# A routed mixture-of-experts kernel: row lists in five groups (1, 1, 2, 4 and 8 experts) instead of three, a third scatter buffer, one gather moved behind later scatters

## The chip, the cores and the metric

The kernel runs on one core of one Trainium2 chip. The metric is the device time of one execution in microseconds (us), lower is better.

## The reference

Input x is 2 x 1024 tokens of 128 channels in f32. A first sublayer (two wavelet levels and linear attention) gives x1; after a layer norm the tokens h go through a routed feed-forward layer, in which each of 16 experts picks its own 256 tokens:

```python
    x = x + _L0_attn_ref(_layernorm(x, axis=-1), ...)
    x = x + _L0_ffn_ref(_layernorm(x, axis=-1), ...)

        scores = jax.nn.sigmoid(h @ gate_w.T)
        cap = math.ceil(T / E * TOP_K)                        # 2048 / 16 * 2 = 256
        topk_score, topk_ids = jax.lax.top_k(scores.T, cap)   # per expert
        xin = h[topk_ids]
        up = jnp.einsum('ecd,efd->ecf', xin, up_w) + up_b[:, None, :]
        g = jnp.einsum('ecd,efd->ecf', xin, gw) + gb[:, None, :]
        eo = jax.nn.silu(g) * up
        eo = jnp.einsum('ecf,edf->ecd', eo, down_w) + down_b[:, None, :]
        flat = (eo * topk_score[..., None]).reshape(-1, Dm)
        out = jnp.zeros_like(h).at[topk_ids.reshape(-1)].add(flat)
        shared = silu(x @ sh_gate_w.T) * (x @ sh_up_w.T)
        return out + shared @ sh_down_w.T
```

The inner width is 512 (four tiles of 128), that of the shared expert 256 (two tiles).

## The kernel before, in words

Each engine (PE, the matmul engine; DVE; ACT; POOL; SP) has its own program, written out by hand, and they meet at semaphores. Nothing is scheduled by a tool: an engine runs its list in order, and a wait holds up all that stands behind it.

**Up to the routing.** The first 82 us make x1, the normalized rows with their scores (stored to DRAM as `h_rows`), and a bitwise search for each expert's 256th highest score. Meanwhile the shared expert runs for the first three quarters of the tokens.

**Row lists.** For every token and expert the rank matmuls leave a slot number, 0 to 255, in PSUM (two copies; ACT copies one to `slot_a`, DVE takes the larger of the two). To turn slots into lists of row numbers, a group of n experts goes through these steps: DVE cuts each slot into a low and a high digit of base 16 and makes one-hot rows of them (`hot_lo`, `hot_hi`), with the token's number multiplied into the low ones (`times_token`); PE multiplies high by low over 16 blocks of tokens into a table of 16n x 16n (`table`, 16 matmuls); DVE keeps the blocks that belong to one expert, sums them and spreads them (`lay_table`, three dependent instructions); PE brings them into slot order (`spread`, one matmul); DVE converts them to integers in `rows` (`slot_rows`). Only then can POOL gather rows for the experts of the group. The groups are of 4, 4 and 8 experts. The steps of group 0 and 1 come before the expert loop, those of group 2 are put between the steps of its first 17 tiles. In the same stretch the shared expert's last quarter is finished (`shared_up`, the product `sh_hid`, `shared_down`, `add_shared`), after which SP stores the last quarter of out.

**Expert loop.** An expert e has four inner tiles j; q = 4e + j counts them. For each q PE does the up and the gate product (L1434, L1435), ACT the silu (L734), DVE the gated product (L1086), and PE two tiles later the down product (L1415). In tile j = 2 PE turns the next expert's gathered rows (`turn_x`, L1402) and DVE copies them (`keep_x`, L1064). When an expert's four down products are done, DVE adds the bias into a buffer `eo` (`add_bias`, L1074), ACT weighs it by the scores (`weigh`, L563, two halves), and POOL scatters it, adding into out (L542, two halves). For the last expert, `add_bias(14)`, `turn_x(15)` and `keep_x(15)` come directly before its tile 60 (`FINAL`).

**POOL's list** sets the order of all gathers and scatters. A gather fetches 128 rows, so there are two per expert and 32 in all, into seven buffers. First come 12 (experts 0 to 5), then per expert its two scatters and `BETWEEN[e]` more gathers:

```python
            def scatter(e):
                if e == 0:
                    pool.wait_ge(s_store, 16 * (NT // 4))
                else:
                    pool.wait_ge(s_scat, 16 * CH * e)
            ...
            for e in range(E):
                scatter(e)
                for _ in range(BETWEEN[e]):
                    gather(*divmod(chunk, CH))
                    chunk += 1
```

So a scatter waits until all scatters before it have landed (they add into the same rows). There are two `eo` buffers: `add_bias(e)` waits until scatter e - 2 has landed.

## Time and profile before

| | |
|---|---|
| median of 3 timed runs | 206.1 us (206.09 to 206.11) |
| profiled execution, first to last instruction | 204.6 us |
| left between the two, around the span | 1.5 us |
| PE busy | 181.2 us (89%), 1196 records |
| DVE busy | 125.5 us (61%) |
| ACT busy | 90.3 us (44%) |
| POOL busy | 127.5 us (62%) |
| mean granted TensorE clock | 0.966 |

The profiled execution has no time of its own besides its span; the 1.5 us by which the timed runs are longer lie outside the first and last instruction. A row of a timeline gives start, duration, engine, line and operation, destination<-source, shape and count, and in brackets the idle time before it with what ended that. PEclk is the granted share of TensorE's full clock (1.00 is 2.4 GHz, 0.50 is 1.2 GHz). Line numbers are those of the kernel before.

### The profile page before, as it was taken

To read this page: it belongs to the slowest core of one execution; us is meant where nothing else is said; L and a number is where in the kernel's file an instruction comes from. 1 tells how busy PE (TensorE), PEld (TensorE's weight loads), DVE (VectorE), ACT (ScalarE), POOL (GpSimd) and SP (SyncE) were. 2 spreads that over 40 slices of the span, in tenths; PEclk is the share of its full clock that TensorE was granted. 3 is DMA by queue.
4 is the path that set the end of the run, shared out by engine and by line. 5 is a ranking of instruction groups with operands and counts; after the bars stand their busy time and mean duration, and the time that the engine had idled before them with its cause. 6 is when DMAs were issued, how large, how long until landed. Compare 5 with 4: busy or idle time off the path is not lost.

```text
span 204.6 us, 3620 instructions
## 1 busy us (share of the span) xinstructions
PE 181.2 (89%) x1196; PEld 156.4 (76%) x1196; DVE 125.5 (61%) x430; ACT 90.3 (44%) x239; POOL 127.5 (62%) x195
## 2 busy tenths in 40 slices
PE   6979898999979999998999999999999999957800
PEld 6947688999936677857899999999999889945700
DVE  4888999999878787785667644454445344422300
ACT  0687512448697768110344344444444345422210
POOL 7494005556117475927777888878878777866660
PEclk9999999999999999999999999999999999995875
DMA  5599999800030271104313323333233333332221
GB/s 149 182 411 419 420 419 419 363 12 3 0 117 0 99 225 51 49 23 138 91 44 42 43 42 45 54 40 42 43 47 53 40 40 29 40 40 21 20 24 13
DMA packets 11649, 22.26 MB, mean 109 GB/s; under 512 B 1504, under 2 KB 8800, under 8 KB 11504
## 3 DMA queue, kind: packets, MB, share of 16 engines
q1 hardware_dynamic: 5968, 17.52, 22.7%
q0 software_dynamic: 5664, 4.53, 16.1%
q8 instruction: 9, 0.15, 0.3%
q14 instruction: 8, 0.07, 0.1%
HBM read 17.72 MB, written 4.33 MB: 108 GB/s over the span
## 4 chain that ended last, share of the span: by engine, by line
PE 41%; DMA 15%; POOL 14%; issue 11%; DVE 10%; ACT 4%; POOLq 1%; SPq 1%; DVEq 0%; ACTq 0%
DMA out_dram<-area,rows 13%; POOL out_dram L542 9%; PE bank L1155 7%; PE bank L1434 4%; PE bank L1110 4%; PE bank L1435 4%; POOL hT L531 4%; PE bank L1296 4%; PE bank L1415 3%; PE bank L1308 3%; DMA x_tok<-in_x_dram 2%; PE bank L1258 2%; DVE junk L950 1%; DVE area L807 1%; DVE hT L817 1%
## 5 line engine op out<-in xcount | busy, mean ns | idle before, releaser
L542 POOL DMA_INDIRECT out_dram<-area,rows x32 | 50.7, 1584 | 16.8 <-DMA out_dram<-area,rows 8.7
L1086 DVE SCALAR_TENSOR_TENSOR area<-bank,consts,sgate 128x256 f32<-128x256 f32 x64 | 30.9, 483 | 42.4 <-ACT sgate L734 42.1
L734 ACT ACTIVATE sgate<-bank,consts 128x256 f32<-128x256 f32 x64 | 30.3, 473 | 53.3 <-PE bank L1435 53.1
L1434 PE MATMUL bank<-area,wT 128*128 128x256 f32 x128 | 40.3, 397 | 4.8 <-issue 4.1
L1415 PEld LDWEIGHTS bank<-wT,area 128*128 128x128 f32 x256 | 38.1, 191 | 4.1 <-DVE area L1086 1.0
L531 POOL DMA_INDIRECT hT<-h_rows,rows x32 | 31.9, 995 | 12.7 <-issue 9.1
L1435 PE MATMUL bank<-area,wT 128*128 128x256 f32 x128 | 39.3, 390 | 0.0
L1415 PE MATMUL bank<-wT,area 128*128 128x128 f32 x256 | 38.6, 275 | 0.6 <-DVE area L1086 0.6
L1435 PEld LDWEIGHTS bank<-area,wT 128*128 128x128 f32 x128 | 25.2, 197 | 3.7
L1434 PEld LDWEIGHTS bank<-area,wT 128*128 128x128 f32 x128 | 20.5, 198 | 6.2 <-issue 5.7
L518 POOL TENSOR_TENSOR sh_hid<-sh_up,sgate 128x64 f32<-128x64 f32 x48 | 13.7, 322 | 14.6 <-ACT sh_up L686 12.1
L1110 PE MATMUL bank<-ident 128*128 128x128 f32 x132 | 19.2, 304 | 1.6 <-POOL ident L411 1.6
L1110 PEld LDWEIGHTS bank<-ident 128*128 128x128 f32 x132 | 17.8, 215 | 2.1 <-POOL ident L411 1.6
L1155 PE MATMUL bank<-sh_hid,area 128*128 128x128 f32 x160 | 18.6, 276 | 0.0
L1155 PEld LDWEIGHTS bank<-sh_hid,area 128*128 128x128 f32 x160 | 18.2, 192 | 0.3 <-ACT area L609 0.3
L1296 PE MATMUL bank<-hT,sh_wT 128*128 128x512 f32 x32 | 17.3, 629 | 0.6 <-ACT hT L650 0.6
L563 ACT ACTIVATE area<-area,hT 128x128 f32<-128x128 f32 x32 | 11.0, 392 | 10.3 <-DVE area L1074 10.3
L950 DVE TENSOR_SCALAR_CACHE_REDUCE junk<-area,search 128x256 bf16<-128x256 f32 (+1 forms) x30 | 13.2, 477 | 1.3 <-ACT area L664 0.8
L491 POOL TENSOR_TENSOR x_tok<-x_tok,consts 128x128 f32<-128x128 f32 x4 | 3.2, 816 | 15.1 <-DVE area L873 15.1
L1074 DVE TENSOR_TENSOR area<-bank,x_tok 128x256 f32<-128x256 f32 x16 | 6.7, 419 | 9.0 <-DMA out_dram<-area,rows 8.2
L1308 PEld LDWEIGHTS bank<-sh_wT,sh_hid 128*128 128x128 f32 x64 | 8.4, 191 | 4.4 <-issue 3.3
L446 POOL TENSOR_TENSOR rstd<-var_eps,half_pow 128x4 f32<-128x4 f32 (+1 forms) x6 | 7.4, 1232 | 6.6 <-DVE var_eps L762 6.6
(195 smaller groups left out, 259.1 us busy)
## 6 DMA issues: line engine op xcount, KB each, us to landing
wT<-in_weights_dram SPq DMA_DIRECT2D x16, 768.0 KB, 16.2
h_rows<-hrow SPq DMA_DIRECT2D x2, 576.0 KB, 3.7
x_tok<-in_x_dram SPq DMA_DIRECT2D x4, 256.0 KB, 3.9
x_tok<-in_down_b_dram SPq DMA_DIRECT2D x1, 1024.0 KB, 6.2
out_dram<-x SPq DMA_DIRECT2D x4, 256.0 KB, 2.1
hT<-h_rows,rows POOLq DMA_INDIRECT x32, 2.6
out_dram<-area,rows POOLq DMA_INDIRECT x32
sh_wT<-in_shared_dram SPq DMA_DIRECT2D x1, 384.0 KB, 2.9
```

The costliest lines, as they stand in the source:

```text
L531: pool.indirect_dma_start(out=gath[:, e % GBUF, c, :], out_offset=None, in_=h_rows[:, :], in_offset=bass.IndirectOffsetOnAxis(ap=rows[:, c ...
L542: pool.indirect_dma_start(out=out_rows, in_=eo[:, e % 2, c, :], in_offset=None, out_offset=bass.IndirectOffsetOnAxis(ap=rows[:, c, e:e + 1 ...
L734: act.activation(sgate_e[:, q % SGB, :], up_bank(q)[:, CAP:2 * CAP], ACT.Silu, bias=biasT[:, 1, j, e:e + 1]).then_inc(s_sil, 1)
L950: last = dve.tensor_scalar(junk[:, k, :], keys, cand[:, k:k + 1], 0.0, ALU.is_ge, ALU.add, accum_out=cnt[:, k:k + 1])
L1086: dve.scalar_tensor_tensor(hidden[:, e % 2, j, :], up_bank(q)[:, 0:CAP], biasT[:, 0, j, e:e + 1], sgate_e[:, q % SGB, :], ALU.add, ALU.mul ...
L1110: pe.matmul(spare[:, 0:P], ident[:, :], ident[:, :], start=True, stop=True)
L1155: last = pe.matmul(dst, band[:, b, m0 + o:m0 + o + P], diag_c[:, d0 - 4 + k, :], start=False, stop=(d0 == 4 and o == 2), skip_group_check= ...
L1296: pe.matmul(bank[2 * kind + t][:, :], sh_wT[:, 2 * kind + t, :], rhs, start=True, stop=True).then_inc((s_shg, s_shu)[kind], 1)
L1308: last = pe.matmul(bank[6 if n == LAST else 4][:, t * P:(t + 1) * P], sh_hid[:, n % 2, k, t * P:(t + 1) * P], sh_wT[:, 4 + k, :], start=(k ...
L1415: last = pe.matmul(bank[3 + e % 2][:, c * P:(c + 1) * P], hidden[:, e % 2, j, c * P:(c + 1) * P], wT[:, e, 2, j, :], start=(j == 0 and c = ...
L1434: pe.matmul(up_bank(q)[:, 0:CAP], wT[:, e, 0, j, :], xselT[:, e % 2, :], start=True, stop=True)
L1435: pe.matmul(up_bank(q)[:, CAP:2 * CAP], wT[:, e, 1, j, :], xselT[:, e % 2, :], start=True, stop=True).then_inc(s_gu, 1)
```

## The change

Four things change. The row lists come in groups of 1, 1, 2, 4 and 8 experts; the two one-expert groups work on the slots of experts 0 and 1 alone (32 columns instead of 256), and for them laying the table is one instruction instead of three. Lists 0 to 2 stand before the expert loop, list 3 (experts 4 to 7) in its tiles 0 and 1, list 4 in tiles 2 to 17. `turn_x(0)` now stands before the last `shared_down`, and two groups of filler matmuls (`stay_warm`, 5 and 3) are gone. A third `eo` buffer lets `add_bias(e)` wait for scatter e - 3. `BETWEEN` moves one gather from behind scatter 7 to behind scatter 12.

```diff
-    BETWEEN = (2, 2, 2, 2, 2, 2, 2, 2, 1, 1, 1, 1, 0, 0, 0, 0)
+    BETWEEN = (2, 2, 2, 2, 2, 2, 2, 1, 1, 1, 1, 1, 1, 0, 0, 0)
...
-        SIZES = (4, 8)
+        SIZES = (1, 2, 4, 8)
...
+        token_1 = sb("token_1", [P, NT], F16)
+        slot_n = sb("slot_n", [P, 2, NT], U16)
+        digit_n = sb("digit_n", [P, 2, 2, NT], U16)
...
-        GROUPS = ((0, 4), (4, 4), (8, 8))
+        GROUPS = ((0, 1), (1, 1), (2, 2), (4, 4), (8, 8))
+        PIECES = (1, 1, 2, 2, 4)
+        NARROW = 2
...
+        def hot_1(flat, g):
+
+            return flat[:, 256 * g:256 * (g + 1)].rearrange("p (a i) -> p a i", a=HI)
...
+        eo_third = carve(CH * C).rearrange("p (c d) -> p c d", c=CH)
...
-        eo = carve(2 * CH * C).rearrange("p (s c d) -> p s c d", s=2, c=CH)
+        eo_two = carve(2 * CH * C).rearrange("p (s c d) -> p s c d", s=2, c=CH)
+        eo = (eo_two[:, 0, :, :], eo_two[:, 1, :, :], eo_third)
+        EOS = len(eo)
...
-            return (bank[6][0:n, 0:n], bank[7][0:n, 0:n], bank[5][0:n, 384:384 + n])[g]
+            return (bank[6][0:n, 0:n], bank[6][0:n, 16:16 + n], bank[7][0:n, 0:n], bank[7][0:n, 64:64 + n],
+                    bank[5][0:n, 384:384 + n])[g]
...
-                    pool.indirect_dma_start(out=out_rows, in_=eo[:, e % 2, c, :], in_offset=None,
+                    pool.indirect_dma_start(out=out_rows, in_=eo[e % EOS][:, c, :], in_offset=None,
...
-            act.copy(by_token(slot_a), ranks[0]).then_inc(s_slota, 1)
+            act.copy(by_token(slot_a)[:, :, :, 0:NARROW], ranks[0][:, :, :, 0:NARROW]).then_inc(s_slota, 1)
+            act.copy(by_token(slot_a)[:, :, :, NARROW:E], ranks[0][:, :, :, NARROW:E]).then_inc(s_slota, 1)
...
-            link(dve.tensor_tensor(by_token(slot_u), by_token(slot_a), ranks[1], ALU.max))
-            link(dve.tensor_scalar(slot_h[:, 1, :], slot_u[:, :], HI - 1, None, ALU.bitwise_and))
+
+            narrow = lambda v: v.rearrange("p e (r k) -> p r k e", r=2)
+            link(dve.tensor_tensor(narrow(slot_n[:, :, :]), by_token(slot_a)[:, :, :, 0:NARROW],
+                                   ranks[1][:, :, :, 0:NARROW], ALU.max))
+            link(dve.tensor_scalar(digit_n[:, 1, :, :], slot_n[:, :, :], HI - 1, None, ALU.bitwise_and))
...
+            def one_hot(k, g):
+
+                return dve.tensor_tensor(hot_1((hi_flat, lo_flat)[k], g).rearrange("p a (j i) -> p a j i", i=8),
+                                         digit_n[:, k, g, :].rearrange("p (j i) -> p j i", i=8).unsqueeze(1).to_broadcast([P, HI, 2, 8]),
+                                         digit[k][:, :, :].unsqueeze(2).to_broadcast([P, HI, 2, 8]), ALU.is_equal)
...
+            def one_times_token(g):
+                return dve.tensor_tensor(hot_1(lo_flat, g), hot_1(lo_flat, g),
+                                         token_1[:, :].unsqueeze(1).to_broadcast([P, HI, NT]), ALU.mult)
...
+            def lay_one(g):
+
+                dve.wait_ge(s_tab, g + 1)
+                dve.tensor_tensor(ext[0:HI, g * P:(g + 1) * P].rearrange("p (b x) -> p b x", x=8),
+                                  table_of(g).unsqueeze(2).to_broadcast([HI, HI, 8]),
+                                  by_x[1][0:HI, :].unsqueeze(1).to_broadcast([HI, HI, 8]), ALU.mult).then_inc(s_spreadL, 1)
...
-            link(hot_lo(0, 0, NT))
-            times_token(0, 0, NT)
-            link(dve.tensor_scalar(slot_h[:, 0, :], slot_u[:, :], 4, None, ALU.logical_shift_right))
+            link(one_hot(1, 0))
+            one_times_token(0)
+            link(dve.tensor_scalar(digit_n[:, 0, :, :], slot_n[:, :, :], 4, None, ALU.logical_shift_right))
+            one_hot(0, 0).then_inc(s_hot, 1)
+            link(one_hot(1, 1))
+            one_times_token(1)
+            lay_one(0)
+            one_hot(0, 1).then_inc(s_hot, 1)
+            slot_rows(0)
+            dve.wait_ge(s_slota, 2)
+            dve.tensor_tensor(by_token(slot_u)[:, :, :, NARROW:E], by_token(slot_a)[:, :, :, NARROW:E],
+                              ranks[1][:, :, :, NARROW:E], ALU.max).then_inc(s_slotu, 1)
+            lay_one(1)
+            dve.wait_ge(s_slotu, 1)
+            for k, (amount, how) in ((1, (HI - 1, ALU.bitwise_and)), (0, (4, ALU.logical_shift_right))):
+                last = dve.tensor_scalar(slot_h[:, k, :].rearrange("p (i e) -> p i e", e=E)[:, :, NARROW:E],
+                                         slot_u[:, :].rearrange("p (i e) -> p i e", e=E)[:, :, NARROW:E], amount, None, how)
+            link(last)
+            slot_rows(1)
+            link(hot_lo(2, 0, NT))
+            times_token(2, 0, NT)
...
-                hot_hi(0, half * NT // 2, (half + 1) * NT // 2)
-            link(hot_lo(1, 0, NT))
-            lay_table(0)
-            slot_rows(0)
-            times_token(1, 0, NT)
-            for half in range(2):
-                hot_hi(1, half * NT // 2, (half + 1) * NT // 2)
-            for t in range(SHT):
+                hot_hi(2, half * NT // 2, (half + 1) * NT // 2)
+
+            def last_hidden(t):
...
+            last_hidden(0)
+            lay_table(2)
+            last_hidden(1)
+            slot_rows(2)
             add_shared(LAST - 1, bank[4])
-            lay_table(1)
-            slot_rows(1)
-            add_shared(LAST, bank[6])
+            link(hot_lo(3, 0, NT))
+            times_token(3, 0, NT)
...
             keep_x(0)
+            for half in range(2):
+                hot_hi(3, half * NT // 2, (half + 1) * NT // 2)
+            add_shared(LAST, bank[6])
...
-                if e >= 2:
-                    dve.wait_ge(s_scat, 16 * CH * (e - 1))
-                dve.tensor_tensor(eo[:, e % 2, :, :], bank[3 + e % 2][:, 0:CAP].rearrange("p (c d) -> p c d", c=CH),
+                if e >= EOS:
+                    dve.wait_ge(s_scat, 16 * CH * (e - EOS + 1))
+                dve.tensor_tensor(eo[e % EOS], bank[3 + e % 2][:, 0:CAP].rearrange("p (c d) -> p c d", c=CH),
...
-                if 1 <= q < 1 + len(LATER):
-                    piece, quarter = LATER[q - 1]
-                    last = piece(2, quarter * NT // 4, (quarter + 1) * NT // 4)
+                if q == 0:
+                    lay_table(3)
+                if q == 1:
+                    slot_rows(3)
+                if 2 <= q < 2 + len(LATER):
+                    piece, quarter = LATER[q - 2]
+                    last = piece(4, quarter * NT // 4, (quarter + 1) * NT // 4)
                     if piece is hot_lo:
                         link(last)
-                if q == 13:
-                    lay_table(2)
-                if q == 16:
-                    slot_rows(2)
+                if q == 14:
+                    lay_table(4)
+                if q == 17:
+                    slot_rows(4)
...
-            shared_up(LAST, 0, 0)
-            stay_warm(WARM_I, bank[7])
...
-                m = HI * GROUPS[g][1]
+                before = sum(PIECES[:g])
                 for i in range(NT):
-                    pieces = 4 if g == 2 else 2
-                    if i % (NT // pieces) == 0:
-                        pe.wait_ge(s_hot, 2 * g + pieces * i // NT + 1)
+                    if i % (NT // PIECES[g]) == 0:
+                        pe.wait_ge(s_hot, before + PIECES[g] * i // NT + 1)
+                    if GROUPS[g][1] == 1:
+                        last = pe.matmul(table_of(g), hot_1(hi_flat, g)[:, :, i], hot_1(lo_flat, g)[:, :, i],
+                                         start=(i == 0), stop=(i == NT - 1))
+                        continue
...
+                if g == 0:
+                    pe.wait_ge(s_slota, 2)
+                else:
+                    pe.wait_ge(s_rows, g)
+                left = g * P if n == 1 else P
...
             table(0)
+            spread(0)
+            table(1)
+            shared_up(LAST, 0, 0)
             shared_up(LAST, 0, 1)
-            spread(0)
+            spread(1)
             shared_up(LAST, 1, 0)
+            pe.wait_ge(s_slotu, 1)
             shared_up(LAST, 1, 1)
-            table(1)
-            pe.wait_ge(s_shsil, SHT * (LAST + 1))
-            for t in range(4):
-                shared_down(LAST, t)
-            spread(1)
-            stay_warm(WARM_E, bank[7])
+            table(2)
+            spread(2)
...
+                if e == 0:
+                    pe.wait_ge(s_lasthid, SHT)
                 if e == 1:
-                    pe.wait_ge(s_rows, 2)
+                    pe.wait_ge(s_rows, 4)
                 if e == 4:
-                    pe.wait_ge(s_spreadL, 3)
+                    pe.wait_ge(s_spreadL, 5)
                 if e == 5:
-                    pe.wait_ge(s_rows, 3)
...
             turn_x(0)
+            for t in range(4):
+                shared_down(LAST, t)
...
-                if q == 13:
-                    table(2)
-                if q == 16:
-                    spread(2)
+                if q == 0:
+                    table(3)
+                if q == 1:
+                    spread(3)
+                if q == 14:
+                    table(4)
+                if q == 17:
+                    spread(4)
```

The order of instructions moves at three places that matter below. PE's list between the last rank matmul and the first product of expert 0 is, before (L1367 is `table`, L1376 `spread`, L1296 `shared_up`, L1308 `shared_down`, L1110 filler, L1402 `turn_x`):

```order
L1308 MATMUL bank<-sh_wT,sh_hid 128x128 x8
L1296 MATMUL bank<-hT,sh_wT 128x512
L1110 MATMUL bank<-ident 128x128 x5
L1367 MATMUL bank<-area 64x64 x16
L1296 MATMUL bank<-hT,sh_wT 128x512
L1376 MATMUL bank<-seat,area 128x8
L1296 MATMUL bank<-hT,sh_wT 128x512 x2
L1367 MATMUL bank<-area 64x64 x16
L1308 MATMUL bank<-sh_wT,sh_hid 128x128 x8
L1376 MATMUL bank<-seat,area 128x8
L1110 MATMUL bank<-ident 128x128 x3
L1402 MATMUL bank<-ident,hT 128x128 x2
```

and after the change, with its own line numbers (L1426 and L1429 `table`, L1443 `spread`, L1357 `shared_up`, L1369 `shared_down`, L1471 `turn_x`):

```order
L1369 MATMUL bank<-sh_wT,sh_hid 128x128 x8
L1426 MATMUL bank<-area 16x16 x16
L1443 MATMUL bank<-seat,area 128x2
L1426 MATMUL bank<-area 16x16 x16
L1357 MATMUL bank<-hT,sh_wT 128x512 x2
L1443 MATMUL bank<-seat,area 128x2
L1357 MATMUL bank<-hT,sh_wT 128x512 x2
L1429 MATMUL bank<-area 32x32 x16
L1443 MATMUL bank<-seat,area 128x4
L1471 MATMUL bank<-ident,hT 128x128 x2
L1369 MATMUL bank<-sh_wT,sh_hid 128x128 x8
```

Three lists stand there instead of two, the 64-column tables are gone, and the last `shared_down` is behind `turn_x(0)`.

PE's first tiles of expert 0 are, before (L1434 and L1435 the up and gate products, L1415 down, L1402 `turn_x(1)`):

```order
L1434 MATMUL bank<-area,wT 128x256
L1435 MATMUL bank<-area,wT 128x256
L1434 MATMUL bank<-area,wT 128x256
L1435 MATMUL bank<-area,wT 128x256
L1434 MATMUL bank<-area,wT 128x256
L1435 MATMUL bank<-area,wT 128x256
L1415 MATMUL bank<-wT,area 128x128 x2
L1402 MATMUL bank<-ident,hT 128x128 x2
```

and after the change (L1505 and L1506 are these products, L1486 down):

```order
L1505 MATMUL bank<-area,wT 128x256
L1506 MATMUL bank<-area,wT 128x256
L1429 MATMUL bank<-area 64x64 x16
L1505 MATMUL bank<-area,wT 128x256
L1506 MATMUL bank<-area,wT 128x256
L1443 MATMUL bank<-seat,area 128x8
L1505 MATMUL bank<-area,wT 128x256
L1506 MATMUL bank<-area,wT 128x256
L1486 MATMUL bank<-wT,area 128x128 x2
```

The table and the spread of experts 4 to 7 now stand between the products of tiles 0, 1 and 2.

POOL's list from the gathers behind scatter 7 to the end is, before (L531 gathers, L542 scatters, each row with its count):

```order
L531 DMA hT<-h_rows,rows 128x144 x2
L542 DMA out_dram<-area,rows 2048x128 x2
L531 DMA hT<-h_rows,rows 128x144
L542 DMA out_dram<-area,rows 2048x128 x2
L531 DMA hT<-h_rows,rows 128x144
L542 DMA out_dram<-area,rows 2048x128 x2
L531 DMA hT<-h_rows,rows 128x144
L542 DMA out_dram<-area,rows 2048x128 x2
L531 DMA hT<-h_rows,rows 128x144
L542 DMA out_dram<-area,rows 2048x128 x8
```

and after the change, from the gather behind scatter 7 (L547 gathers, L558 scatters):

```order
L547 DMA hT<-h_rows,rows 128x144
L558 DMA out_dram<-area,rows 2048x128 x2
L547 DMA hT<-h_rows,rows 128x144
L558 DMA out_dram<-area,rows 2048x128 x2
L547 DMA hT<-h_rows,rows 128x144
L558 DMA out_dram<-area,rows 2048x128 x2
L547 DMA hT<-h_rows,rows 128x144
L558 DMA out_dram<-area,rows 2048x128 x2
L547 DMA hT<-h_rows,rows 128x144
L558 DMA out_dram<-area,rows 2048x128 x2
L547 DMA hT<-h_rows,rows 128x144
L558 DMA out_dram<-area,rows 2048x128 x6
```

Behind scatter 7 stands one gather instead of two, and behind scatter 12 stands one, the second half of expert 15, where none stood.

## Rows read from the trace of the kernel before

**Rows 1.** The page's part 4: the chain that ended last, share by engine

```profile
PE 41%; DMA 15%; POOL 14%; issue 11%; DVE 10%; ACT 4%; POOLq 1%; SPq 1%; DVEq 0%; ACTq 0%
```

**Rows 2.** POOL's timeline: start, duration, line, operation, idle before and its releaser

```profile
90.26 1.14 POOL L531 DMA_INDIRECT hT<-h_rows,rows  x1 [3.28 <-DVE rows L1032]
...
105.51 1.63 POOL L542 DMA_INDIRECT out_dram<-area,rows  x1 [0.30 <-issue]
...
112.54 1.62 POOL L542 DMA_INDIRECT out_dram<-area,rows  x1 [0.70 <-ACT area L563]
...
157.52 1.63 POOL L542 DMA_INDIRECT out_dram<-area,rows  x1 [0.30 <-ACT area L563]
...
177.71 1.01 POOL L531 DMA_INDIRECT hT<-h_rows,rows  x1 [0.30 <-issue]
179.54 1.58 POOL L542 DMA_INDIRECT out_dram<-area,rows  x1 [0.81 <-DMA out_dram<-area,rows]
181.42 1.56 POOL L542 DMA_INDIRECT out_dram<-area,rows  x1 [0.30 <-issue]
...
195.62 1.55 POOL L542 DMA_INDIRECT out_dram<-area,rows  x1 [1.95 <-DMA out_dram<-area,rows]
```

**Rows 3.** DVE's timeline, columns as before

```profile
89.81 0.17 DVE L1032 CAST rows<-bank 128x8 uint32<-128x8 f32 x1 [0.52 <-PE bank L1376]
...
96.09 0.42 DVE L1064 COPY area<-bank 128x256 f32<-128x256 f32 x1 [0.32 <-PE bank L1402]
98.39 0.48 DVE L1086 SCALAR_TENSOR_TENSOR area<-bank,consts,sgate 128x256 f32<-128x256 f32 x1 [1.87 <-ACT sgate L734]
...
184.72 0.42 DVE L1074 TENSOR_TENSOR area<-bank,x_tok 128x256 f32<-128x256 f32 x1 [3.33 <-DMA out_dram<-area,rows]
...
194.00 0.42 DVE L1074 TENSOR_TENSOR area<-bank,x_tok 128x256 f32<-128x256 f32 x1 [0.80 <-PE bank L1415]
```

**Rows 4.** PE's timeline; xN counts merged records, two for an f32 matmul

```profile
83.80 2.00 PE L1308 MATMUL bank<-sh_wT,sh_hid 128*128 128x128 f32 x16
...
87.71 0.69 PE L1367 MATMUL bank<-area 128*64 128x64 f16 x16
...
89.39 0.39 PE L1376 MATMUL bank<-seat,area 64*128 64x8 f32 x2
...
96.66 0.67 PE L1434 MATMUL bank<-area,wT 128*128 128x256 f32 x2 [0.61 <-DVE area L1064]
...
98.46 0.59 PE L1434 MATMUL bank<-area,wT 128*128 128x256 f32 x2
...
161.60 0.38 PE L1402 MATMUL bank<-ident,hT 128*128 128x128 f32 x2
...
164.22 0.67 PE L1434 MATMUL bank<-area,wT 128*128 128x256 f32 x2 [0.92 <-issue]
...
185.58 1.19 PE L1434 MATMUL bank<-area,wT 128*128 128x256 f32 x2 [3.21 <-issue]
```

**Rows 5.** ACT's timeline, weighing (L563) of experts 1 and 15

```profile
111.35 0.68 ACT L563 ACTIVATE area<-area,hT 128x128 f32<-128x128 f32 x2
...
194.46 0.69 ACT L563 ACTIVATE area<-area,hT 128x128 f32<-128x128 f32 x2 [1.78 <-DVE area L1074]
```

**Rows 6.** Groups of DVE instructions by shape: count, busy us, mean ns

```profile
L1013 DVE TENSOR_TENSOR area<-area,digit 128x512 f16<-128x512 uint16 x8 | 3.2, 419 | 0.0
...
L1038 DVE TENSOR_TENSOR x<-bank,x 128x512 f32<-128x512 f32 x2 | 1.4, 680 | 0.0
```

**Rows 7.** The page's part 5, a group of POOL: count, busy us, mean ns, idle before

```profile
L491 POOL TENSOR_TENSOR x_tok<-x_tok,consts 128x128 f32<-128x128 f32 x4 | 3.2, 816 | 15.1 <-DVE area L873 15.1
```

**Rows 8.** DMA issues in 160 to 182 us: us from issue to landing

```profile
hT<-h_rows,rows POOLq DMA_INDIRECT x4, 2.6
```

**Rows 9.** Stretches: busy PE, PEld, DVE, ACT, POOL; PEclk; DMA

```profile
183.50:184.00 0.50, 0.00 (x0) 0.00 (x0) 0.00 (x0) 0.00 (x0) 0.00 (x0) 0.71 1.05 90
...
190.50:191.00 0.50, 0.50 (x5) 0.47 (x4) 0.00 (x0) 0.11 (x1) 0.50 (x1) 0.97 0.00 0
```

8 lines of the change are left out of this document (6 added, 2 removed).

## The prediction

> **What bounds the kernel now.** Read the chain that ended last first: PE has 41% of it, then scatters and POOL, with 15% and 14% [rows 1]. PE's share is the part up to about 112 us; from there to the end the chain is scatters. The timeline of POOL says why. Expert 0's scatter starts at 105.51, with POOL never idle behind the twelve gathers before it; expert 1's starts at 112.54, and here POOL sat idle 0.70 us, for ACT's weighing of expert 1 [rows 2]. That is the last time that the expert loop holds POOL up. From 112.54 to 157.52 seven intervals with two gathers between scatters take 6.43 us each; four with one gather, from there to 179.54, take 22.02, so 5.505 each; three without a gather, to 195.62, take 16.08, so 5.36 each [rows 2]. With one gather or none, POOL is idle before the next scatter, for the landing of the one before it (0.81 and 1.95 us): the landing sets the interval, and a single gather is nearly hidden in it. With two it is POOL's own issuing that sets it.
>
> In the other engines' timelines the reader is to see that PE is ahead of POOL: DVE's bias addition for expert 14 waited 3.33 us for a scatter to free its buffer, and PE stood idle 3.21 us before expert 15 because of it [rows 3, 4]. In that idle time TensorE's granted clock went from 2.4 to 1.2 GHz, at about 183.8, and it came back at about 190.5 (a mean of 0.71 in the first stretch, of 0.97 in the second) [rows 9]. So expert 15 took from 185.58 to 194.00, 8.42 us, 4.9 of them at half clock; at full clock it would be 8.42 - 2.47 = 5.95. Its weighing starts at 194.46, the first half takes about 0.39 and POOL needs some 0.32 more, so the last scatter could have started at 195.17; it started at 195.62, held by the landing of scatter 14 [rows 2, 5]. What counts is the start of that scatter; what follows it stays as it is.
>
> **The change, term by term.** The profiled span is 204.6 us, the median 206.1; the 1.5 between them lie outside the span, and I add the difference to the median.
>
> *First lists.* PE's `shared_down` before the tables ends at 85.8, and DVE's six small instructions for expert 0 (0.17 to 0.42 each) should by then be done [rows 3, 4, 6]. A table of 64 columns took 0.69, 39 ns for each of 16 matmuls [rows 4]; I keep 0.62 for the 16-column one. The Trainium skill (TensorE: Matmul & The Clock Gate, section "Wait — 56ns, not 53.3ns?") says that matmuls start no closer than about 25 ns however few their columns; by it such a table takes 0.40, and the loop would begin some 0.4 earlier. No row here shows a 16-column table. From the end of a table to the first gather it took 90.26 - 88.40 = 1.86; two of three laying instructions, about 0.25 each, drop out. So the first gather starts at 86.4 + 1.36 = 87.8, 2.5 us earlier. Lists 1 and 2 come behind spreads (0.39), another table, and four `shared_up`, which stream 512 columns where a product streams 256 in 0.45 (two tiles, four products, take 98.46 - 96.66 = 1.80), so 0.87 each [rows 4]. On PE: spread 0 at 86.9 (after the laying), table 1 to 87.7, two `shared_up` to 89.45, spread 1 to 89.85, two more to 91.4, table 2 to 92.0. DVE lays it by 92.85, spread 2 is done at 93.3, and list 2 is there at 93.5, so gathers for experts 2 and 3 start at 93.8, 0.9 after POOL is free.
>
> *Start of the expert loop.* `turn_x(0)` waits for the last `sh_hid`, at 93.45. DVE has then `add_shared` (0.68), a one-hot and a token product of 1,024 columns (0.7 each, less than twice the 0.42 of 512) and `keep_x(0)` (0.42) [rows 3, 6]; with some 0.1 saved at each overlap the copy ends at 95.9 and PE starts at 96.0, against 96.66. PE's own list (two transposes, 1.85 of `shared_down`) ends at 95.65, so DVE sets it. That lead is spent at once. Between tiles 0 and 1 stands table 3 (0.62), between 1 and 2 spread 3. The gated product of tile 0 ends 2.2 after the tile's start (96.66 to 98.39 + 0.48) [rows 3, 4], so at 98.2; three laying instructions bring 98.95; the spread starts at 99.0, while PE is through tile 1 at 98.4. Behind that wait stand tile 2, and with it all later tiles. Tile 2 starts at 99.2, against 98.46 before: 0.75 later [rows 4]. Bounds: tables at no cost and each DVE step 0.1 shorter give 98.4; every new DVE step at its 512-column price and no overlap give 100.0.
>
> *First scatters.* List 3 is there at 99.75, so POOL starts expert 4's gathers at 100.0, idles some 1.2 us for it, and could scatter expert 0 at 105.0. Expert 1 decides: its weighing, first half, was done at 111.35 + 0.39 = 111.74, with 0.32 to POOL 112.06, and 0.75 later that is 112.8 [rows 5]. So scatter 1 starts at 112.8, 0.3 later than before; the early first gather buys nothing. The bounds of tile 2 give 112.0 to 113.6.
>
> *The gather that moves.* After the change there are six intervals with two gathers (38.55), six with one (33.03) and two with none (10.72): 82.3 us instead of 83.1 [rows 2]. POOL by itself comes to scatter 15 at 112.8 + 82.3 = 195.1, 0.5 earlier than before.
>
> *The third buffer.* It takes away DVE's waits for scatters, 3.33 at the longest, and PE can run at its pace. But what stands behind is late next: the last gather. It was issued at 177.71, long before it was needed; now it stands behind scatter 12. That one starts at 112.8 + 38.55 + 27.5 = 178.9, its second half 1.88 later, the gather 1.86 after that (1.56 and 0.30 of issue), at 182.6, and it lands 2.6 later, at 185.2 [rows 2, 8]. Two transposes and the copy take about 1.05, so expert 15 starts at 186.3, 0.7 later than before. PE, which turned expert 12 at 161.60 and needs 5.47 per expert, is there by 182, so it waits as long as before, and its clock can fall as before [rows 4, 9]. With 5.95 to 8.42 for the expert and 1.17 to the scatter, scatter 15 could start between 193.4 and 195.9. I take the middle, 194.65, since the idle time is about the same but nothing fixes when the clock comes back. It lies under 195.1, so POOL's chain sets the end.
>
> *No cost.* The added constants are 17 small instructions on POOL during the setup. Behind them POOL sits idle for 15.1 us; its 128-column additions take 0.816 each, so even at that price they would be 13.9 and stay covered [rows 7]. Without that idle time they would delay the first norms by as much. The two filler groups on PE (eight matmuls) stood in waits. The last store of out is issued near 97.3, some eight microseconds before scatter 0 waits for it.
>
> Sum: scatter 15 at 195.1 instead of 195.62: 206.1 - 0.5 = **205.6 us**.
>
> **The rivals.**
> *The late gather sets the end.* If expert 15 again needs 8.42, scatter 15 starts at 195.9: 206.4; it decides from 7.6 on. For it speaks the same idle time before the expert, against it that the clock need not stay low as long. 205.7 to 206.4.
> *Slower: list 3 holds the loop up.* PE waits inside the loop for a list that DVE can lay only after the gated product of tile 0. If tile 2 starts 1.6 late, at 100.1 or later, scatter 1 moves to 113.7 and scatter 15 to 196.0: 206.5; each further microsecond is one more. For it: three dependent DVE steps and two hand-overs to PE, each of which I took at its shortest; against it, the steps have rows.
> *Slower: the clock falls in the list stage.* The fillers are gone, and PE waits some 0.5, 0.9 and 0.6 us. A wait of 0.92 at 164 went by at full clock, one of 1.4 did not [rows 4, 9]. At the price of expert 15, up to 2.5 us, less the gain: 208.1 at most.
> *Faster than forecast: the lead holds.* If small tables and one-hots cost half, tile 2 starts as before and scatter 1 at 112.0 to 112.2: 204.9.
>
> **How the numbers follow.** Forecast 0.50 (205.1 to 206.1), late gather 0.20, the slower ones 0.20 together, the lead 0.10. A measurement of this kernel tells 0.2%, 0.4 us, from no change. Faster by more than that: 0.35 of the forecast and the lead, 0.45. Within it: 0.15 of the forecast, 0.17 of the late gather and a little of the slower ones, 0.35. Slower: 0.20. The range goes from 204.7, where the lead holds, to 207.0, above the late gather and a list that comes a microsecond later than I count.
>
> **What would show it.** Right, if in the new profile POOL's first gather starts near 87.8, PE idles before spread 3 and starts its third tile near 99.2, scatter 1 waits for ACT until about 112.8, eight intervals between scatters of 5.4 to 5.5 follow six of 6.4, DVE's bias additions wait for no scatter, and PE idles for the last gather. Wrong, if the granted clock falls before 100 us, if scatter 1 comes after 113.7, or if the last scatter waits for ACT instead of a landing.

## The result, and the profile after

The changed kernel takes 210.3 us (median of 4 runs, 209.1 to 210.8) beside 206.1 of the kernel before: a ratio of 1.020, with a 95% interval of 1.018 to 1.022. The prediction was 205.6, with a range from 204.7 to 207.0. The profiled execution has a span of 209.1 us instead of 204.6, and scatter 15 starts at 200.03 instead of 195.62: 4.41 us to explain.

The page's part 4, the chain that ended last, after the change (it answers to [rows 1]):

```profile
PE 65%; DVE 11%; DMA 7%; ACT 5%; POOL 5%; issue 3%; POOLq 1%; SPq 1%; DVEq 0%; ACTq 0%
```

The view puts PE on the chain up to about 172 us, because at scatters 7 to 11 it names ACT's weighing as what POOL waited for. ACT's timeline after shows that this is not so:

```profile
155.43 0.68 ACT L579 ACTIVATE area<-area,hT 128x128 f32<-128x128 f32 x2
160.89 0.68 ACT L579 ACTIVATE area<-area,hT 128x128 f32<-128x128 f32 x2
```

These are the weighings of experts 8 and 9. Scatter 8 starts at 161.71, 6.28 us after its own weighing; that of expert 9 just happened to start shortly before it. The other thing that a scatter waits for is the landing of the one before it. So the experts don't hold POOL up there. From scatter 3 on its own issuing and the landings set the intervals as in the kernel before (6.43 with two gathers, about 5.45 with one), and what is late by then stays late. POOL's timeline after (to [rows 2]):

```profile
88.22 0.95 POOL L547 DMA_INDIRECT hT<-h_rows,rows  x1 [1.49 <-DVE rows L1069]
...
115.93 1.62 POOL L558 DMA_INDIRECT out_dram<-area,rows  x1 [1.23 <-ACT area L579]
...
122.33 1.62 POOL L558 DMA_INDIRECT out_dram<-area,rows  x1 [0.30 <-issue]
...
127.91 1.02 POOL L547 DMA_INDIRECT hT<-h_rows,rows  x1 [2.08 <-DVE rows L1069]
...
156.25 1.63 POOL L558 DMA_INDIRECT out_dram<-area,rows  x1 [0.30 <-ACT area L579]
...
161.71 1.58 POOL L558 DMA_INDIRECT out_dram<-area,rows  x1 [0.62 <-ACT area L579]
...
183.46 1.58 POOL L558 DMA_INDIRECT out_dram<-area,rows  x1 [0.64 <-DMA out_dram<-area,rows]
...
187.20 1.02 POOL L547 DMA_INDIRECT hT<-h_rows,rows  x1 [0.30 <-issue]
...
200.03 1.55 POOL L558 DMA_INDIRECT out_dram<-area,rows  x1 [2.12 <-DMA out_dram<-area,rows]
```

The first gather starts 2.0 us earlier (2.5 were forecast), and yet scatter 1 starts 3.39 later. Scatters 2 and 7 are 122.33 and 156.25; a wait of 2.08 for list 4, which the kernel before had ready at 121, makes the six intervals from scatter 1 to scatter 7 1.76 us longer than the 38.56 of before. From scatter 7 to 8 the moved gather saves 0.96, the next four save 0.27 together, and the last three cost 0.49 more. So 3.39 + 1.76 - 0.96 - 0.27 + 0.49 = 4.41.

PE's timeline after (to [rows 4]; L1357 is `shared_up`, L1369 `shared_down`, L1426 and L1429 `table`, L1471 `turn_x`, L1505 the up product):

```profile
83.78 2.00 PE L1369 MATMUL bank<-sh_wT,sh_hid 128*128 128x128 f32 x16
86.27 0.71 PE L1426 MATMUL bank<-area 128*16 128x16 f16 x16 [0.49 <-DVE area L1016]
87.36 0.38 PE L1443 MATMUL bank<-seat,area 16*128 16x2 f32 x2 [0.37 <-DVE area L1027]
...
88.30 2.92 PE L1357 MATMUL bank<-hT,sh_wT 128*128 128x512 f32 x4
...
91.66 2.45 PE L1357 MATMUL bank<-hT,sh_wT 128*128 128x512 f32 x4
...
98.41 0.67 PE L1505 MATMUL bank<-area,wT 128*128 128x256 f32 x2
...
101.68 0.70 PE L1505 MATMUL bank<-area,wT 128*128 128x256 f32 x2
...
120.13 1.06 PE L1429 MATMUL bank<-area 128*128 128x128 f16 x16
122.31 0.41 PE L1471 MATMUL bank<-ident,hT 128*128 128x128 f32 x2 [1.12 <-DVE area L1062]
...
189.75 0.44 PE L1471 MATMUL bank<-ident,hT 128*128 128x128 f32 x2 [2.44 <-DMA hT<-h_rows,rows]
190.76 0.67 PE L1505 MATMUL bank<-area,wT 128*128 128x256 f32 x2 [0.56 <-issue]
```

Four `shared_up` took 2.92 and 2.45 for two each, where the kernel before has 1.98 for two. The stretches say why (to [rows 9], same columns):

```profile
88.00:89.00 1.00, 1.00 (x14) 0.73 (x12) 0.76 (x4) 0.00 (x0) 0.79 (x1) 1.00 0.00 0
...
89.00:89.50 0.50, 0.50 (x2) 0.22 (x2) 0.00 (x0) 0.00 (x0) 0.20 (x2) 0.72 0.00 0
...
90.00:91.00 1.00, 1.00 (x2) 0.00 (x0) 0.00 (x0) 0.20 (x1) 0.42 (x1) 0.50 0.11 28
...
92.50:93.00 0.50, 0.50 (x2) 0.19 (x1) 0.47 (x3) 0.00 (x0) 0.50 (x1) 0.87 0.00 0
93.00:94.00 1.00, 1.00 (x3) 0.19 (x1) 1.00 (x3) 0.60 (x1) 0.69 (x2) 1.00 0.00 0
...
192.00:195.00 3.00, 3.00 (x8) 2.34 (x8) 0.97 (x2) 0.95 (x2) 0.74 (x2) 0.50 0.25 22
```

TensorE was at 1.2 GHz from about 89.2 to 92.6, after PE had stood idle 0.49 us (before 86.27) and 0.37 us (before 87.36), and DVE stood idle behind it, 2.90 us for spread 1 (to [rows 3] and [rows 5], DVE and then ACT):

```profile
91.84 0.16 DVE L1069 CAST rows<-bank 128x2 uint32<-128x2 f32 x1 [2.90 <-PE bank L1443]
...
198.41 0.42 DVE L1131 TENSOR_TENSOR area<-bank,x_tok 128x256 f32<-128x256 f32 x1 [0.80 <-PE bank L1486]
```

```profile
114.74 0.68 ACT L579 ACTIVATE area<-area,hT 128x128 f32<-128x128 f32 x2
...
198.87 0.69 ACT L579 ACTIVATE area<-area,hT 128x128 f32<-128x128 f32 x2 [1.78 <-DVE area L1131]
```

No bias addition waits for a scatter any more. The weighing of expert 1 starts 1.19 us before its scatter; in the kernel before it was also 1.19 (111.35 and 112.54, [rows 2, 5]).

### The profile page after: what moved, and what is told of

It is laid out like the page before. It is cut to its first block, busy times and chain, and to the rows that moved or that the text cites. A ratio compares the mean times of both kernels' runs of the same rounds, so it can differ in the third digit from the quotient of the medians.

```text
span 209.1 us, 3697 instructions
## 1 busy us (share of the span) xinstructions
PE 183.2 (88%) x1216; PEld 156.5 (75%) x1216; DVE 128.3 (61%) x445; ACT 90.2 (43%) x240; POOL 132.5 (63%) x212
## 4 chain that ended last, share of the span: by engine, by line
PE 65%; DVE 11%; DMA 7%; ACT 5%; POOL 5%; issue 3%; POOLq 1%; SPq 1%; DVEq 0%; ACTq 0%
PE bank L1505 12%; PE bank L1486 11%; PE bank L1506 11%; PE bank L1216 7%; PE bank L1357 5%; POOL out_dram L558 4%; DMA out_dram<-area,rows 3%; PE bank L1171 3%; DMA x_tok<-in_x_dram 2%; PE bank L1369 2%; PE bank L1471 2%; PE bank L1319 2%; DVE junk L967 1%; DMA hT<-h_rows,rows 1%; DVE area L824 1%
## 5 line engine op out<-in xcount | busy, mean ns | idle before, releaser
L558 POOL DMA_INDIRECT out_dram<-area,rows x32 | 50.7, 1583 | 17.3 <-ACT area L579 5.9
L547 POOL DMA_INDIRECT hT<-h_rows,rows x32 | 32.1, 1004 | 16.6 <-DVE rows L1069 8.4
L1486 PEld LDWEIGHTS bank<-wT,area 128*128 128x128 f32 x256 | 38.1, 192 | 3.9 <-DVE area L1143 0.8
L1505 PE MATMUL bank<-area,wT 128*128 128x256 f32 x128 | 39.8, 393 | 0.8 <-issue 0.6
L1506 PE MATMUL bank<-area,wT 128*128 128x256 f32 x128 | 39.0, 387 | 0.0
L1486 PE MATMUL bank<-wT,area 128*128 128x128 f32 x256 | 38.6, 275 | 0.4 <-DVE area L1143 0.4
L1506 PEld LDWEIGHTS bank<-area,wT 128*128 128x128 f32 x128 | 24.9, 194 | 3.6
L1505 PEld LDWEIGHTS bank<-area,wT 128*128 128x128 f32 x128 | 20.0, 195 | 1.9 <-issue 1.5
L1357 PE MATMUL bank<-hT,sh_wT 128*128 128x512 f32 x32 | 18.5, 676 | 0.6 <-ACT hT L666 0.6
L1171 PE MATMUL bank<-ident 128*128 128x128 f32 x116 | 17.5, 313 | 1.6 <-POOL ident L425 1.6
L1171 PEld LDWEIGHTS bank<-ident 128*128 128x128 f32 x116 | 16.3, 224 | 1.6 <-POOL ident L425 1.6
L1369 PEld LDWEIGHTS bank<-sh_wT,sh_hid 128*128 128x128 f32 x64 | 8.4, 191 | 4.0 <-issue 2.9
L1471 PE MATMUL bank<-ident,hT 128*128 128x128 f32 x32 | 6.3, 278 | 5.5 <-DMA hT<-h_rows,rows 4.1
L694 ACT ACTIVATE below<-area,search 128x256 bf16<-128x256 f32 (+1 forms) x15 | 7.6, 508 | 4.8 <-DVE search L981 4.0
```

Source lines behind the costliest of these rows:

```text
L547: pool.indirect_dma_start(out=gath[:, e % GBUF, c, :], out_offset=None, in_=h_rows[:, :], in_offset=bass.IndirectOffsetOnAxis(ap=rows[:, c ...
L558: pool.indirect_dma_start(out=out_rows, in_=eo[e % EOS][:, c, :], in_offset=None, out_offset=bass.IndirectOffsetOnAxis(ap=rows[:, c, e:e + ...
L1171: pe.matmul(spare[:, 0:P], ident[:, :], ident[:, :], start=True, stop=True)
L1357: pe.matmul(bank[2 * kind + t][:, :], sh_wT[:, 2 * kind + t, :], rhs, start=True, stop=True).then_inc((s_shg, s_shu)[kind], 1)
L1486: last = pe.matmul(bank[3 + e % 2][:, c * P:(c + 1) * P], hidden[:, e % 2, j, c * P:(c + 1) * P], wT[:, e, 2, j, :], start=(j == 0 and c = ...
L1505: pe.matmul(up_bank(q)[:, 0:CAP], wT[:, e, 0, j, :], xselT[:, e % 2, :], start=True, stop=True)
```

## The experiments

One table holds the runs. Three columns count from the start of the `shared_down` group before the lists (83.80 before, 83.78 after), which takes out what happened earlier: the first product of expert 0, tile 2, and scatter 1. The next one goes from scatter 1 to scatter 15. The last is the granted clock in the list stage of the profiled execution. All columns from the fourth on are of that one execution; the medians and ratios are of several.

| kernel | us | ratio, 95% interval | first product | tile 2 | scatter 1 | 1 to 15 | clock |
|---|---|---|---|---|---|---|---|
| before | 206.1 | | 12.86 | 14.66 | 28.74 | 83.08 | 1.00 |
| after | 210.3 | 1.020 (1.018, 1.022) | 14.63 | 17.90 | 32.15 | 84.10 | fell |
| e1 fillers | 210.1 | 1.019 (1.014, 1.024) | 13.35 | 16.60 | 30.85 | 84.88 | 1.00 |
| e2 list 4 | 209.6 | 1.017 (1.011, 1.024) | 13.03 | 16.28 | 30.52 | 84.11 | 1.00 |
| e4 lists alone | 211.3 | 1.026 (1.020, 1.031) | 13.03 | 16.28 | 30.52 | 84.67 | 1.00 |
| e5 fillers, list 4 | 208.0 | 1.008 (1.006, 1.011) | 13.35 | 16.61 | 30.84 | 83.81 | 1.00 |
| e12 work first, list 4 | 210.1 | 1.011 (1.002, 1.020) | 14.32 | 17.51 | 31.74 | 84.18 | fell |
| e17 order, list 4 | 208.0 | 1.008 (1.005, 1.011) | 12.48 | 15.74 | 29.98 | 83.68 | 1.00 |
| e19 the same, old gathers | 209.9 | 1.019 (1.014, 1.023) | 14.03 | 17.28 | 31.51 | 83.92 | fell |
| e18 e5, setup fillers | 209.2 | 1.011 (1.006, 1.016) | 13.35 | 16.60 | 30.83 | 84.34 | 1.00 |
| e3 before + tail | 205.6 | 0.998 (0.994, 1.001) | 12.86 | 14.66 | 28.74 | 82.57 | 1.00 |
| e13 before + gather | 206.6 | 1.000 (0.996, 1.003) | 12.86 | 14.66 | 28.75 | 83.58 | 1.00 |
| e6 before + buffer | 206.5 | 1.000 (0.997, 1.004) | 12.86 | 14.66 | 28.75 | 83.20 | 1.00 |
| e9 before + buffer, gather first | 209.5 | 1.013 (1.007, 1.019) | 12.86 | 14.66 | 29.37 | 85.83 | 1.00 |
| e10 before, no fillers | 207.1 | 1.001 (0.997, 1.004) | 12.07 | 13.87 | 27.96 | 85.43 | 1.00 |
| e14 e3, no fillers | 206.3 | 1.000 (0.998, 1.002) | 12.06 | 13.86 | 27.95 | 83.96 | 1.00 |
| e15 e3, second fillers out | 207.0 | 1.000 (0.996, 1.005) | 12.45 | 14.25 | 28.33 | 83.82 | 1.00 |
| e16 e6, no fillers | 206.3 | 0.998 (0.995, 1.000) | 12.32 | 14.13 | 28.21 | 84.00 | 1.00 |

The ratios are to the kernel before on the same chip (206.1 to 206.5 us); they are as recorded and not the quotients of two medians. From tile 2 to scatter 1 it is 14.23 to 14.25 us in every kernel with the new lists and 14.08 to 14.09 in every one with the old but e9, where POOL is late by itself (14.71). In all others scatter 1 follows PE's tile 2 at a fixed distance.

**e1: fillers back.** In PE's list:

```diff
+            stay_warm(3, bank[7])
             table(0)
+            stay_warm(2, bank[7])
             spread(0)
```

> The changed kernel with fillers back in the list stage: three filler matmuls before table 0 and two between table 0 and spread 0, where PE stood idle 0.49 and 0.37 us. Clock theory: the granted clock stays at 1.00 from 88 to 95 us instead of 0.50 to 0.69 in between, the two pairs of shared_up take 1.98 us each instead of 2.92 and 2.45, the first product comes some 1.4 us earlier, near 97.0, tile 2 near 100.3, scatter 1 near 114.5, scatter 15 about 1.4 earlier: 208.9 us. Rival, that the dearer small DVE steps and the waits for each list set the loop's start and the clock's fall is covered by them: the first product moves by less than 0.4 us and the time stays at 210. Rival that the fillers get in the way: table 0 and the first gather come up to 0.5 us later, 210.5.

The clock stayed at 1.00, the `shared_up` pairs took 1.98, and the first product came 1.28 earlier than after the change. The rival of a covered fall is out. But the median hardly moved (210.1 beside 210.3). Two things bear on that. Behind scatter 1 the profiled e1 lost 0.8 us to the changed kernel, most of it in one interval (last section). And the changed kernel's runs go from 209.1 (mean clock 0.972) to 210.8 (0.966, the profiled one), which would fit a clock that doesn't fall every time; but a run without a profile doesn't show it, since the mean clock also counts falls near the end (e6 has 0.964 with a full clock in the list stage). So the price of the fall is shown for the profiled execution, and its share in the median isn't.

**e2: list 4 one tile earlier**, as the last list stands in the kernel before.

```diff
-                if 2 <= q < 2 + len(LATER):
-                    piece, quarter = LATER[q - 2]
+                if 1 <= q < 1 + len(LATER):
+                    piece, quarter = LATER[q - 1]
...
-                if q == 14:
+                if q == 13:
                     table(4)
-                if q == 17:
+                if q == 16:
                     spread(4)
```

> The changed kernel with every step of list 4 (one-hots, table, laying, spread, rows) one tile earlier, at the tiles where the kernel before has them for its last list: table at tile 13, spread at tile 16, in front of nothing that waits for the laying. Theory that list 4's place costs on its own: PE's idle 1.12 us before turn_x(4) and POOL's idle 2.08 us before the first gather of expert 8 go away, scatter 3 comes about 1.8 us earlier (128.7) and, since PE's pace sets the scatters from 161 us on, scatter 15 about 1.2 earlier: 209.1 us; scatter 1 stays near 115.9. Rival, that the late last gather or the landing of the scatters takes the gain back: scatter 3 is earlier, but scatter 15 by less than 0.3, 210.0 us.

POOL's timeline of e2 at the first gather of expert 8:

```profile
124.26 1.02 POOL L547 DMA_INDIRECT hT<-h_rows,rows  x1 [0.30 <-issue]
```

Its wait of 2.08 and PE's of 1.12 are gone: from scatter 1 to scatter 3 it takes 12.87 us instead of 14.59. But from scatter 1 to 15 it takes 84.11, as in the changed kernel (84.10). Of the 1.72 gained, 1.36 are lost again in the interval before scatter 10 (6.79 instead of 5.43, last section), so in this execution the rival has it; and PE's pace, from which the theory took its 1.2, doesn't set the scatters there. In this execution the clock did not fall, without any filler. PE's timeline of e2:

```profile
88.00 1.98 PE L1357 MATMUL bank<-hT,sh_wT 128*128 128x512 f32 x4
...
96.51 0.67 PE L1505 MATMUL bank<-area,wT 128*128 128x256 f32 x2
...
99.76 0.70 PE L1505 MATMUL bank<-area,wT 128*128 128x256 f32 x2
```

So e2 gives the list stage at full clock, to the hundredth the same as e4: scatter 1 at 30.52, 1.78 later than before; with the low clock it was 32.15. The fall cost 1.63.

**e4: the lists alone**: `eo` with two buffers and `BETWEEN` as before.

> The changed kernel with two scatter buffers and the gathers spread as before: the change of the lists alone. Theory that the lists carry the whole loss: scatter 1 near 115.9, list 4 held at 127.5 as in the changed kernel, and a time of 209.8 to 210.6. Rival, that the moved gather carries a part: expert 15's turn no longer waits 2.4 us for a gather and scatter 15 starts 1 us or more before that of the changed kernel, 209.2 or less. Rival, that the third buffer gave something back: bias additions wait for scatters again, as the 3.33 us of before, and the time is above 211.

The lists carry the loss: alone they lose as much as the whole change, as far as the intervals tell (1.020 to 1.031 beside 1.018 to 1.022). The third rival's time came out, and so did its waits, up to 3.4 us. But in the profiled execution, the fastest with 209.4, each scatter from scatter 9 on waits for a landing (1.96 us for the last) and none for ACT, so these waits are not what cost it there; its other runs, up to 212.5, have no profile.

**e3: the tail alone**, on the kernel before: the third buffer and the new `BETWEEN`.

> The kernel before with only the third buffer and the moved gather, its lists as they were. The prediction's terms for these two: scatter 1 stays at 112.54, six intervals of 6.43, six of 5.505 and two of 5.36 bring scatter 15 to 194.8, no bias addition waits for a scatter, and the time is 0.8 us less than before, 205.3. Rival, the late gather sets the end: the last gather lands near 185, PE idles for it, the clock falls and expert 15 takes its 8.4 us, so scatter 15 starts at 195.6 to 195.9: 206.1 to 206.4. Theory that the moved gather alone accounts for a part of the loss of the changed kernel: 207 or more.

82.57 from scatter 1 instead of 83.08, and POOL's timeline of e3 at scatter 15:

```profile
194.73 1.55 POOL L545 DMA_INDIRECT out_dram<-area,rows  x1 [2.47 <-ACT area L566]
```

The moved gather saves 0.98 in its interval (0.93 forecast), and the late gather then holds scatter 15 for ACT, which costs 0.53 in the last interval. The late-gather rival names this wait, though not its size. The ten times fall in two groups: six from 205.2 to 205.7 with a mean clock of 0.971 to 0.976, four from 206.5 to 207.2 with 0.965 to 0.967.

**e13: only the moved gather; e6: only the buffer.**

> The kernel before with only the moved gather: two scatter buffers, the old lists. Theory that the third buffer is what lets the moved gather pay: bias additions wait for scatters as before (3.33 us for expert 14), the last gather lands after that, expert 15 starts late in both cases, and scatter 15 starts at 195.2 or later: 205.8 to 206.8 us, slower than the 205.6 with the buffer. Rival, that the buffer is worth nothing: the time equals that of the gather and the buffer together, 0.5 us under the kernel before.

> The kernel before with the third buffer alone. Theory that the chain of scatters sets the end and the buffer only moves a wait: scatter 1 and all intervals as before, scatter 15 within 0.2 us of 195.6, 206.1 us, with no bias addition waiting for a scatter and expert 15 done earlier. Rival, that earlier weighing saves part of each landing-bound interval: 205.6 or less.

Both came out within the numbers of the first theory, and neither can be told from no change. Without the buffer scatter 15 of e13 started at 195.96, after 3.38 us of waiting for ACT; with the buffer alone (195.41) no bias addition waits for a scatter and the landings set the end as they did. The intervals of e3 and e13 overlap, so it is not shown that the buffer makes the gather pay, nor that the two together gain.

**e10: the kernel before without its fillers.**

```diff
-            stay_warm(WARM_I, bank[7])
...
-            stay_warm(WARM_E, bank[7])
```

> The kernel before without its two groups of filler matmuls (five before table 0, three before turn_x of expert 0), all else as it was. Theory that the fillers held the clock: PE waits about 1.2 us for the one-hots of list 0 and the granted clock falls below 1.00 between 86 and 93 us, in the profiled execution or in some of the others; scatter 1 comes up to 1.9 us later where it falls, and the median is 207 to 208. Rival, that the fillers stood in waits and are worth nothing: the clock stays at 1.00, the first product of expert 0 moves by less than 0.1 us and the time is that of the kernel before.

Neither holds. The clock stayed at 1.00 in the profiled execution with idle times of 0.58 and 0.91 us in PE, and the first product came 0.79 earlier: the fillers did not stand in waits, they stood on PE's way. The median did not follow (1.001); in the profiled execution two scatter intervals took 7.11 and 7.01 us (last section).

**e12: real work in place of fillers, and list 4 earlier.** The order is `shared_up(LAST, 0, 0)`, `table(0)`, `shared_up(LAST, 0, 1)`, `spread(0)`, `table(1)`, `shared_up(LAST, 1, 0)`, `spread(1)`.

> The changed kernel with both of its losses treated: the first shared_up stands before table 0, the second before spread 0, the third before spread 1, so that PE has work where it waited 0.5 and 0.4 us, and list 4 has its steps one tile earlier. Theory that the clock, the waits in the list stage and list 4's place carry the loss: the granted clock stays at 1.00, the first product of expert 0 comes 0.5 us or more earlier than the 96.5 of the last run with a full clock, tile 2 near 99.2, scatter 1 near 113.3, no wait for list 4, and the time is 207.5 us or less. Rival, that DVE's chain of list steps sets tile 2 whatever PE does: tile 2 stays at 99.7 or later and the time near 208.7.

PE's timeline of e12, `shared_down` before the loop:

```profile
94.68 3.50 PE L1369 MATMUL bank<-sh_wT,sh_hid 128*128 128x128 f32 x16
```

The rival is right and goes further. Table 2 came at 92.16 as in e2 (92.13), because DVE wasn't ready; PE's idle time moved to there (0.54, 0.84 and 0.31 us), and the clock fell there instead: 3.50 for what takes 1.95.

**e17: the order around list 2.** DVE makes list 2's one-hots before it waits for spread 1, and PE's `table(2)` stands before the last two `shared_up`; list 4 as in e2.

> The changed kernel with list 4 one tile earlier and the order around list 2 changed: DVE makes the one-hots of list 2 before it waits for spread 1, where it stood idle 1.76 us (2.90 with the low clock), and PE has table 2 before the last two shared_up, so that DVE lays it meanwhile. Theory that two engines wait for each other in the list stage: table 2 starts near 90.3 instead of 92.1, PE's idle 0.79 before spread 2 goes, turn_x of expert 0 comes near 93.6 instead of 94.2, the first product near 95.9 instead of 96.5, scatter 1 near 113.4, and the time is 207 to 207.7. Rival, that PE's work sets the stage whatever the order: the first product stays at 96.3 or later and the time at that of the kernel with list 4 alone moved.

Table 2 at 89.96, the first product 12.48 behind `shared_down`: 0.55 less than in e2 and 0.38 less than in the kernel before, so the two engines did wait for each other. Yet tile 2 is still 1.08 later than before: tiles 0 and 1 take 3.26 us instead of 1.80, for table 3 and spread 3 between them.

**e5: fillers and list 4.**

> The changed kernel with the fillers before table 0 and spread 0 and, with them, list 4 one tile earlier. If the fall of the clock and list 4's place are two separate losses, both go: the clock stays at 1.00 until 100 us, scatter 1 stands near 114.2, POOL waits for no list behind scatter 2, scatter 15 starts near 197.5 and the time is about 208.3, with what is left over the kernel before, some 1.5 to 2 us, in the list stage and in tiles 0 and 1. Rival, that what list 4 gives back is lost again to late landings at the end: 209.5 or more.

Its median is 208.0, 2.2 below e1, which lacks only the move of list 4. In the profiles each edit takes away its own loss: the clock stays at 1.00, and scatter 2 to 3 takes 6.41 instead of 8.19. The medians don't add up that way: the fillers alone gained 0.1%, list 4 alone 0.3%, both 1.2%, more than half of the whole. The times of e2 may hide a fall of the clock in two of its four runs (mean clock 0.959 and 0.958, those of the others 0.972 and 0.966); they have no profile.

**e19: e17 with the old gathers.**

> The changed kernel with list 4 one tile earlier and the new order around list 2, and the gathers spread as in the kernel before: the last gather behind scatter 11. Theory that the moved gather gains only its 0.8 to 1.0 us in the interval behind scatter 7 and loses it at the end, where expert 15 waits for it with a low clock: the time equals that of the same kernel with the moved gather, 207.5 to 208.5, and expert 15 waits for no gather. Rival, that the moved gather is still worth something: 208.8 or more; rival, that it costs: 207.2 or less.

It can't be read as meant. In the profiled e19 the clock fell in the list stage, with the same instructions there as in e17; its four runs have a lower mean clock (0.950 to 0.960, those of e17 0.961 to 0.973). The two also ran on different chips, so a difference between chips is not ruled out. PE's timeline of e19, first `shared_up` pair:

```profile
88.28 3.30 PE L1357 MATMUL bank<-hT,sh_wT 128*128 128x512 f32 x4
```

What it does show is the price of the fall once more: the first product 1.55 later than in e17.

**Attempts to beat both kernels: e9, e14, e15, e16.** e9 is the kernel before with the third buffer, `AHEAD = 13` and one gather behind scatter 7.

> The kernel before with the third buffer and its lists as they were, but the gather moved the other way: 13 gathers before scatter 0 instead of 12, and one behind scatter 7 instead of two. Scatter 0 comes 1.25 us later (106.4), scatter 1, which waited 0.70 for ACT, about 0.3 later (112.8), then six intervals of 6.43, five of 5.5 and three of 5.36 bring scatter 15 to 194.9 or 195.0, with expert 15 there in time since the last gather is issued before scatter 12: 205.4 us, at or under the kernel with the gather behind scatter 12, whose last scatter waited 2.47 us for ACT. Rival, that scatter 1 is later by the whole 1.25 less nothing: 113.4 and 206.0 us.

It was 209.5 us (1.013, interval 1.007 to 1.019) for a reason that neither theory had: the shifted gathers reach expert 8 before scatter 2, and POOL stood 3.66 us for the last list, ahead of that scatter. e14 is e3 without fillers, e15 e3 without the second group only, e16 e6 without fillers.

> The kernel before with the third buffer and the moved gather, its old lists, and without the two groups of fillers in the list stage. Without fillers the first product of expert 0 came 12.1 us after the last shared_down of the quarter before, instead of 12.9, and scatter 1 0.8 us earlier; the buffer and the gather were worth 0.5. If both hold together: scatter 1 near 111.7 and scatter 15 near 193.9, 204.8 us, faster than both kernels. Rival, that the late gather and the landings take the earlier start back: 205.5 or more, the same as the kernel before.

> The same, but with the first group of fillers (five, before table 0) kept and only the second (three, before turn_x of expert 0) taken out. The five cost 0.46 us, since without them table 0 came that much earlier; the three cost the other 0.33. Scatter 1 near 112.1, scatter 15 near 194.3, 205.1 us; if the fillers before table 0 hold up the clock in some executions, the spread of its times is smaller than without them.

> The kernel before with the third buffer and without the fillers of the list stage; gathers and lists as they were. Theory that the late gather is what makes the end uncertain: with the last gather back behind scatter 11, PE waits for nothing before expert 15, the last scatter waits for a landing and not for ACT, and the times lie close together. Scatter 1 near 111.5, seven intervals with two gathers, four with one, three with none: 82.3 to 83.1 from scatter 1, scatter 15 near 194.6, 205.1 us. Rival, that a transfer which delays a landing by 1 us or more takes it back: 206 or more, with one interval between 153 and 175 us above 6 us where 5.5 is usual.

e14 starts 0.8 earlier and ends no earlier; e15 is 207.0, with two runs at 204.8 and 205.0 and the others above 206.3, a wider spread than that of e14 and not a smaller one: in its profiled execution the last scatter waited 3.64 us for an expert 15 that was at half clock to 191.1. e16 lies closer together (205.3 to 206.8) and its interval just touches 1; as its rival had it, one interval was long (7.24 instead of 6.42, scatter 7 to 8). None can be told from the kernel before.

**e18: eight more fillers in the setup of e5**, to move a load of instructions (last section).

> The changed kernel with fillers and with list 4 moved, and eight more filler matmuls in the setup, in a place where PE stood idle 1.25 us: nothing changes but how far PE is in its program. In the runs so far a scatter's interval is 0.6 to 1.5 us longer than usual where a load of instructions (16 KB) comes 3 to 4 us after that interval's first scatter issue, and is as usual where it comes within 2.5 us or where there is none. If the load is PE's, it comes some 2 us earlier, near 166.3 instead of 168.5, and the interval before scatter 10, 6.65 us in the profiled run without these fillers, falls to 5.5: 207.0 us instead of 208.0. Rival, that the load isn't PE's or has no part in it: the load stays where it was, or it moves and the long interval stays.

The load moved, further than expected (161.4 instead of 168.5, where 166.3 was forecast), which speaks for PE's but leaves the distance unexplained, and the interval before scatter 10 was 5.50 instead of 6.65. But the fillers made the whole of the list stage 1 us later, in the profiled execution the last scatter waited 3.72 us for ACT (an interval of 7.13), and the median, 209.2, shows no gain.

## Why the prediction was wrong

- **"First lists", first gather at 87.8:** nearly right, 0.4 late: 4.4 us behind the start of `shared_down` instead of 4.0 (88.22 and 83.78; the same in e2 and e4), because PE stood some 0.48 for the one-hots of list 0, which the step had as done by then. The early gather is, as it said, worth nothing. A 16-column table takes 0.64 from its start to what follows, 40 ns for each matmul, as the 64-column ones: the value kept was right. The Trainium skill (TensorE: Matmul & The Clock Gate, section "Wait — 56ns, not 53.3ns?") gives about 25 ns as the least; these tables don't come near it.
- **"Start of the expert loop", first product at 96.0:** mis-sized by 0.8 at full clock (13.03 behind `shared_down` instead of 12.2). That is the 0.48 that PE stands for the first one-hots, counted at nothing, and four `shared_up` at 0.96 instead of 0.87 (0.36 together). The other waits, 0.37, 0.79 and 0.31 in e2, were counted at about their size. The sum also has a slip: 89.85 and two times 0.87 make 91.6, not 91.4. Tiles 0 and 1 with list 3 were forecast at 3.2 and took 3.25 to 3.27.
- **"The two filler groups on PE stood in waits":** the step that failed first. They were on PE's way (0.8 us, e10), and without them the clock fell in three of the six profiled executions with the new lists (after, e12 and e19; not e2, e4 and e17), with them in none of three (e1, e5, e18). A fall cost 1.63 us (after against e2) or 1.55 (e19 against e17). That would fit fillers that hold the clock, but it doesn't settle it: PE's waits before it were the same with and without a fall (0.48 and 0.37 us in e17 and e19), and the kernel before kept its clock without fillers too (e10, e14, e16). This was a rival, with its mechanism and a price of up to 2.5, but it shared a chance of 0.20 with another.
- **"First scatters", scatter 1 at 112.8:** even at tile 2's own time it was 0.5 short, because the step used 0.71 from weighing to scatter where [rows 2, 5] give 1.19 in the kernel before. At full clock scatter 1 is 1.78 later than before: 0.17 to the first product, 1.45 in tiles 0 and 1, 0.16 behind them. The rival "list 3 holds the loop up", from tile 2 at 100.1 on, is what happens even at full clock.
- **List 4:** no term at all, and no reason given. Its steps come one tile later than the last list of before; 1.76 us at POOL.
- **"The gather that moves", 0.8, and "the third buffer":** right in that no bias addition waits for a scatter, that the gather saves 0.96 where it stood, and that the last gather is late next. That the sum is close as well (0.96 + 0.27 - 0.49 = 0.74) is in part luck: neither the 0.27 of the next four intervals nor the 0.49 of the last three was foreseen. Expert 15 took 7.65 from start to bias addition, inside the 5.95 to 8.42; the gather lands 2.5 us after its issue (2.6 in [rows 8]). But the 0.71 stood here too. Where a profile names ACT at the last scatter, that scatter starts 1.16 after its weighing starts (e3, e13, e15, e18), and the same 1.16 stands in the kernel before (194.46 and 195.62). So there expert 15 and the landing of scatter 14 were done at nearly the same time, with no 0.45 us between them, and a late expert 15 sets the end from 7.2 us on, not from 7.6. In e3 it did.
- **"No cost", the constants:** right; POOL's idle time before the additions of [rows 7] is 10.2 us instead of 15.1.

Sum for the profiled execution: lists at full clock 1.78, clock 1.63, list 4 1.76, tail -0.74, and -0.02 from an earlier start: 4.41. The clock's share is that of this execution; the profiled one of e4, without the fall, took 209.4. What stays open is why the clock falls in e19 and not in e17, and in the changed kernel and not in e2 and e4, with the same instructions on PE in that stage.

## What to carry to other kernels

A list cut into smaller groups costs the engine that makes the tables once per group, and a smaller table is hardly cheaper (0.64 us for 16 columns, 0.49 for 32, 0.62 for 64): before cutting, count the cost per group on the engine that sets the next stage, here PE and not POOL. When pieces are renumbered, price every piece, also the last one that only shifts by a tile, by who waits for it. And a filler is either cover for a wait or work on the path; which of the two is seen when it is taken out.

## What the runs showed of the hardware

**Loads of instructions coincide with late scatters.** Each profile has a few loads of 16 KB (q8 in the DMA view, about 1.1 us of one DMA engine). In e5 one fell at 168.5, 4.3 us after the first half of scatter 9 was issued. The DMA queues of e5 from 168 to 169, and POOL's timeline:

```profile
q8 instruction: 1, 0.02, 6.8%
```

```profile
164.24 1.58 POOL L558 DMA_INDIRECT out_dram<-area,rows  x1 [0.64 <-DMA out_dram<-area,rows]
166.13 1.56 POOL L558 DMA_INDIRECT out_dram<-area,rows  x1 [0.30 <-issue]
167.99 1.02 POOL L547 DMA_INDIRECT hT<-h_rows,rows  x1 [0.30 <-issue]
170.89 1.58 POOL L558 DMA_INDIRECT out_dram<-area,rows  x1 [1.88 <-DMA out_dram<-area,rows]
```

The wait for the landing is 1.88 instead of 0.6 to 0.8, the interval 6.65 instead of 5.4 to 5.6. Over the 18 profiles, intervals with one gather in which the load came 3.2 to 4.8 us after the first half took 5.92 to 7.03 (e1, e2, e5, e10, e12, e14, e17, e19); where it came within 3.2 us, or there was none, 5.34 to 5.64. With two gathers, where POOL's own issuing sets the 6.42, three such loads went with 6.99 to 7.24 (e9, e10, e16) and four with 6.43 to 6.45 (after, e1, e5, e18). The changed kernel has one more load in the end, near 192, and its interval from scatter 13 to 14 was 5.70 instead of 5.37. The Trainium skill (Runtime: NRT & Kernel Launch, section "Instruction fetch mechanics") calls the cost of such a refill mostly hidden; here it goes with a later landing of a scatter that the next one waits for. That the load is the cause rests on this coincidence in time, which e18 supports but doesn't settle.

**Small DVE operations aren't cheap by their size.** DVE by shape, after the change (count, busy us, mean ns):

```profile
L1016 DVE TENSOR_TENSOR area<-digit_n,digit 128x256 f16<-128x256 uint16 x4 | 1.3, 335 | 0.1
...
L1012 DVE TENSOR_SCALAR digit_n<-slot_n 128x32 uint16<-128x32 uint16 x1 | 0.5, 541 | 0.0
```

The first digit of 32 columns took 0.52 to 0.54 us in six profiles, where the kernel before has 0.28 for 256 columns, and a one-hot of 256 columns 0.27 to 0.49 beside 0.42 for 512 [rows 6].
